# Layer 0's edge stage: running sums carried by a matmul with the identity, and copied out by ScalarE

## What is computed

```
e = einsum('ehd,ehd->eh', q[src], k[dst]) * scale
m = segment_max(e, dst);  ex = exp(e - m[dst]);  denom = segment_sum(ex, dst)
agg = segment_sum(ex / denom[dst] * v[src], dst)
```

## Time and profile before

| | |
|---|---|
| median of 3 runs | 6235.39 us (6235.18 to 6241.73) |
| the profiled execution | 6232.7 us |
| its span, first to last instruction | 6230.8 us |
| granted TensorE clock, mean of the span | 0.838 |
| the changed stage | about 727 to 2160 us, a quarter of the span |

### The profile page before, as it was taken

One profiled execution on the slowest core, in us unless ns is written; L12 is line 12 of the kernel. 1 busy time (PEld: TensorE's weight loads), 2 busy tenths in 40 slices (PEclk: granted clock), 3 DMA queues, 4 the chain that ended last, 5 costly groups with the idle time before them and its releaser, 6 DMA issues. The chain is left out here.

```text
span 6230.8 us, 86151 instructions
## 1 busy us (share of the span) xinstructions
PE 4655.4 (75%) x21453; PEld 3370.4 (54%) x21454; DVE 3982.9 (64%) x9527; ACT 2668.4 (43%) x5421; POOL 3080.8 (49%) x3260
## 2 busy tenths in 40 slices
PE   6977577777777697499999225566556659999999
PEld 4753255555555597366666215444444436666665
DVE  6864389999999777232222777777777764444443
ACT  1541055555555432154444212767776632222222
POOL 2767366666666487577777001777777720000000
PEclk7989899989899855599999557777777779999999
DMA  2014678888888686333232227555555530000000
GB/s 57 1 28 119 227 236 250 249 249 246 250 248 251 205 200 166 99 80 79 65 79 66 77 64 232 154 151 149 151 151 150 150 102 12 12 12 12 5 7 12
DMA packets 587385, 787.21 MB, mean 126 GB/s; under 512 B 207700, under 2 KB 427323, under 8 KB 586749
## 3 DMA queue, kind: packets, MB, share of 16 engines
q0 software_dynamic: 159136, 383.90, 23.0%
q1 hardware_dynamic: 290173, 351.82, 17.8%
q10 hardware_dynamic: 137972, 50.36, 3.3%
HBM read 634.22 MB, written 158.32 MB: 127 GB/s over the span
## 5 line engine op out<-in xcount | busy, mean ns | idle before, releaser
L1372 POOL DMA_INDIRECT b_got<-tmp_l_table,b_src x928 | 878.6, 947 | 505.8 <-issue 256.2
L2473 POOL DMA_INDIRECT w_got<-tmp_l_table,w_src x928 | 881.9, 950 | 284.4 <-issue 277.2
L3216 POOL DMA_INDIRECT t_got<-tmp_f_table,t_src x672 | 634.4, 944 | 220.4 <-issue 202.7
L1616 PE MATMUL b_pk<-b_keys,b_hot_t 128*128 x1856 | 532.9, 437 | 249.7 <-issue 157.2
L2736 PE MATMUL w_pa<-w_got,w_hot 128*128 128x264 f32 x1856 | 589.7, 471 | 98.8 <-DVE w_got L2643 96.5
L1616 PEld LDWEIGHTS b_pk<-b_keys,b_hot_t 128*128 128x128 f32 x1856 | 377.8, 214 | 335.2 <-issue 280.8
L3667 DVE SCALAR_TENSOR_TENSOR l_accs<-l_po,l_prob,l_accs 128x256 f32 (+1 forms) x392 | 173.5, 480 | 566.8 <-PE l_po L3776 566.8
L3719 ACT ACTIVATE l_h<-l_ph,l_bn 128x896 f32<-128x896 f32 x224 | 245.0, 1096 | 655.6 <-PE l_ph L3766 655.6
L2736 PEld LDWEIGHTS w_pa<-w_got,w_hot 128*128 128x128 f32 x1856 | 406.2, 231 | 205.2 <-issue 120.3
L1631 PE MATMUL b_pa<-b_got,b_hot 128*128 128x260 f32 x1856 | 487.7, 410 | 5.6 <-DVE b_acc L1543 4.8
L1631 PEld LDWEIGHTS b_pa<-b_got,b_hot 128*128 128x128 f32 x1856 | 387.0, 209 | 77.4 <-issue 7.0
(11 more groups left out here) (579 smaller groups left out, 9980.2 us busy)
## 6 DMA issues: line engine op xcount, KB each, us to landing
tmp_g_acc<-b_acc SPq DMA_DIRECT2D x232, 260.0 KB, 3.6
b_spread<-tmp_g_rel_rows SPq DMA_DIRECT2D x116, 256.0 KB, 5.3
w_spread<-tmp_g_rel_rows SPq DMA_DIRECT2D x116, 256.0 KB, 3.5
e_attr<-in_edge_attr ACTq DMA_DIRECT2D x103, 256.0 KB, 4.4
tmp_f_experts<-t_y SPq DMA_DIRECT2D x28, 896.0 KB, 4.5
t_spread<-tmp_f_rel_rows SPq DMA_DIRECT2D x174, 128.0 KB
yl_y<-tmp_f_experts SPq DMA_DIRECT2D x20, 896.0 KB, 11.2
b_got<-tmp_l_table,b_src POOLq DMA_INDIRECT x928, 4.5
```

The source lines that it names most:

```text
L1372: pool.indirect_dma_start(out=got[:, m % NB, u, :], out_offset=None, in_=T["l0_table"], in_offset=bass.IndirectOffsetOnAxis(ap=src[:, m * ...
L1616: mm = pe.matmul(pk[:, b % 2, u * D:(u + 1) * D], hot_t[:, (at * B4 + b) % HB, u * P:(u + 1) * P], keys[:, bass.ds(tile[u // 2], 1), :], s ...
L2473: pool.indirect_dma_start(out=got[:, p % 3, u, :], out_offset=None, in_=T["l1_table"], in_offset=bass.IndirectOffsetOnAxis(ap=src[:, p * R ...
L3216: pool.indirect_dma_start(out=got[:, g % RING, u, :], out_offset=None, in_=T["f_table"], in_offset=bass.IndirectOffsetOnAxis(ap=src[:, g * ...
```

## The change

The running sum is no longer made by VectorE. TensorE leaves a stop's bank open after the two sums (`sum_of_stop`) and adds a third matmul, `carry_of_stop`: the identity times one of six rows of `sums`, picked by a register: the four places of acc, faded_acc (4) or zeros (5). ScalarE copies the finished bank to acc (`collect`) and raises `added`. The row's number stands beside the numbers of tiles in a new table `orders`, 16 values a round, worked out once by VectorE from keep; TensorE loads all 16 at the head of a round. keep is loaded to one partition. TensorE's order interleaves carries and the next stop's sums; the last copy of a round (stop 7) opens ScalarE's next round; VectorE's `fade_last` moves behind score 0. The calls of the rounds get or lose the argument `two_behind`.

```diff
+    FADED, NONE = AS, AS + 1
...
-        keep = s.sb("keep", [P, L.stops])
+        keep = s.sb("keep", [1, L.stops])
+        orders = s.sb("orders", [1, ROUNDS + 1, 2 * RS], I32)
...
-        acc = s.sb("acc", [P, AS, WV])
-        faded_acc = s.sb("faded_acc", [P, WV])
+        sums = s.sb("sums", [P, AS + 2, WV])
+        acc, faded_acc = sums[:, 0:AS, :], sums[:, FADED, :]
...
-            sp.dma_start(keep[:, :], T[L.name + "_keep"].partition_broadcast(P)).then_inc(loaded, 16)
+            sp.dma_start(keep[:, :], T[L.name + "_keep"].rearrange("(a s) -> a s", a=1)).then_inc(loaded, 16)
+            sp.dma_start(orders[0:1, 0:ROUNDS - 2, 0:RS], T[L.name + "_i_row"][RS + 2:RS * (ROUNDS - 1) + 2]
+                         .rearrange("(a p s) -> a p s", a=1, s=RS)).then_inc(loaded, 16)
+            sp.dma_start(orders[0:1, ROUNDS - 2, 0:RS - 2], T[L.name + "_i_row"][RS * (ROUNDS - 1) + 2:L.stops]
+                         .rearrange("(a s) -> a s", a=1)).then_inc(loaded, 16)
...
+            def collect(p, n):
+                g = p * RS + n
+                if n % 2 == 0 and (not isinstance(p, int) or p or n >= AS):
+                    act.wait_ge(stored[n // 2 % 2], 16 * (RS // AS * p + n // AS))
+                act.wait_ge(summed, g + 1)
+                act.activation(acc[:, n % AS, :], pa[:, n % 2, 0:WV], ACT.Copy).then_inc(added, 1)
...
+                if two_behind:
+                    collect(p - 2, RS - 1)
...
+                collect_of(0)
                 if behind:
                     make_hot(p - 1, 2)
                     make_apart(p - 1, 3)
+                collect_of(1)
                 if two_ahead:
                     make_hot_t(p + 2, at + 2, 1)
+                collect_of(2)
...
+                collect_of(3)
+                collect_of(4)
+                if now_:
...
+                collect_of(5)
                 if two_ahead:
                     make_hot_t(p + 2, at + 2, 2)
+                collect_of(6)
...
+            dve.memset(sums[:, NONE, :], 0.0)
+            dve.wait_ge(loaded, 96)
+            for n in range(RS):
+                before = FADED if n == 0 else (n - 1) % AS
+                dve.tensor_scalar(orders[0:1, 1:ROUNDS + 1, RS + n], keep[0:1, :].rearrange("a (p s) -> a p s", s=RS)[:, :, n],
+                                  float(before - NONE), float(NONE), ALU.mult, ALU.add)
...
                 weigh_of(0)
-                if two_behind:
-                    add(p - 2, at - 2, RS - 2)
-                    add(p - 2, at - 2, RS - 1)
+                score_of(0)
                 if behind:
                     fade_last(p - 1)
-                score_of(0)
                 if now_:
                     spans(p)
...
+            def orders_of(p, a, b):
+                return values(orders[0:1, bass.ds(p, 1), a:b].rearrange("a p s -> a (p s)"))
...
+            def sum_of_stop(p, n, k):
+                g, b = p * RS + n, n // 2
+                pe.wait_ge(hot_ready, p * B4 + b + 1)
+                pe.wait_ge(rhs_ready, p * B4 + b + 1)
+                if not isinstance(g, int) or g >= 2:
+                    pe.wait_ge(added, g - 1)
+                for u in range(2):
+                    v = 2 * (n - 2 * b) + u
+                    pe.matmul(pa[:, n % 2, 0:WV], hot[:, b, v, :], got[:, k, v, D:ROW], start=(u == 0), stop=False)
+            def carry_of_stop(p, n, value):
+                before = nc.s_assert_within(value, 0, NONE, skip_runtime_bounds_check_because="it is worked out from a comparison's 0 or 1")
+                if n == 0:
+                    pe.wait_ge(faded, p + 1)
+                else:
+                    pe.wait_ge(added, p * RS + n)
+                pe.matmul(pa[:, n % 2, 0:WV], K["ident"][:, :], sums[:, bass.ds(before, 1), :], start=False, stop=True).then_inc(summed, 1)
...
-                    tile = tiles(p + 1, 2, 10 if two_ahead else 8)
+                first, last = 0 if ahead else RS, 2 * RS if behind else RS
+                if ahead and not two_ahead:
+                    tile, kept = orders_of(p, 0, RS - 2), orders_of(p, RS, 2 * RS)
+                else:
+                    found = orders_of(p, first, last)
+                    tile, kept = found[0:RS - first], found[RS - first:]
                 expand_of(1)
-                sums_of(0, 0, 1)
+                sum_of(0)
+                carry_of(0)
+                sum_of(1)
                 if now_:
                     chain_ends(p)
                 expand_of(2)
-                sums_of(1, 2, 3)
+                carry_of(1)
+                sum_of(2)
+                carry_of(2)
+                sum_of(3)
                 if now_:
                     spread_tops(p)
                 expand_of(3)
-                sums_of(2, 4, 5)
+                carry_of(3)
+                sum_of(4)
+                carry_of(4)
+                sum_of(5)
                 if now_:
                     turn_weights(p)
                 expand_of(4)
-                sums_of(3, 6, 7)
-
-            pe.wait_ge(loaded, 64)
+                carry_of(5)
+                sum_of(6)
+                carry_of(6)
+                sum_of(7)
+                carry_of(7)
+            pe.wait_ge(set_up, 2)
+            pe.wait_ge(loaded, 96)
             pe.wait_ge(keys_in[0], 16)
-            tile = tiles(0, 0, 10)
+            tile = values(i_row[0:1, 0:RS + 2])
```

More of the change, by code:

```diff
@@ L1400, in make_hot, with round_, collect_of @@
                 act.activation(hot[:, b, :, :], apart[:, b % 2, :, :], ACT.Relu, scale=-1.0, bias=K["ones"][:, 0:1]).then_inc(hot_ready, 1)
-            def round_(p, at, two_ahead, ahead, now_, behind):
+            def round_(p, at, two_ahead, ahead, now_, behind, two_behind):
+                def collect_of(n):
+                    if behind:
+                        collect(p - 1, n)
+                if two_behind:
+                    collect(p - 2, RS - 1)
                 if ahead:
@@ L1436, in _ @@
             act.wait_ge(set_up, 2)
-            round_(0, 0, True, True, True, False)
-            round_(1, 1, True, True, True, True)
+            round_(0, 0, True, True, True, False, False)
+            round_(1, 1, True, True, True, True, False)
             with act.Fori(0, TIMES) as i:
                 for c in range(LOOP):
[L1441 to L1444, removed]
+                    round_(LOOP * i + 2 + c, 2 + c, True, True, True, True, True)
+            round_(ROUNDS - 2, ROUNDS - 2, False, True, True, True, True)
+            round_(ROUNDS - 1, ROUNDS - 1, False, False, True, True, True)
+            round_(ROUNDS, ROUNDS, False, False, False, True, True)
+            round_(ROUNDS + 1, ROUNDS + 1, False, False, False, False, True)
         @block.vector
@@ L1530, in weigh, with round_ @@
                 dve.tensor_tensor(rows, rows, w.unsqueeze(3).broadcast_to((P, U, H, V)), ALU.mult).then_inc(rhs_ready, 1)
[L1532 to L1546, removed]
+            def round_(p, at, turn, ahead, now_, behind):
                 def weigh_of(b):
@@ L1554, in score_of @@
                         score(p + 1, at + 1, b, slot(at + 1, b), turn + (B4 * (at + 1) + b) // NB)
[L1556 to L1559, removed]
                 if behind:
@@ L1588, in _ @@
             done = link.here
-            round_(0, 0, 0, True, True, False, False)
+            round_(0, 0, 0, True, True, False)
             done = link.here - done
-            round_(1, 1, 0, True, True, True, False)
+            round_(1, 1, 0, True, True, True)
             with dve.Fori(0, TIMES) as i:
@@ L1594, in _, with values @@
                 for c in range(LOOP):
-                    round_(LOOP * i + 2 + c, 2 + c, i, True, True, True, True)
+                    round_(LOOP * i + 2 + c, 2 + c, i, True, True, True)
             link.leave(TIMES)
[L1597 to L1600, removed]
+            round_(ROUNDS - 2, ROUNDS - 2, 0, True, True, True)
+            round_(ROUNDS - 1, ROUNDS - 1, 0, False, True, True)
+            round_(ROUNDS, ROUNDS, 0, False, False, True)
         @block.tensor
         def _(pe):
-            def tiles(p, a, b):
-                return nc.values_load_multi_w_load_instructions(i_row[0:1, bass.ds(p * RS + a, b - a)], engines=[mybir.EngineType.PE],
+            def values(row):
+                return nc.values_load_multi_w_load_instructions(row, engines=[mybir.EngineType.PE],
                                                                 min_val=0, max_val=NT - 1, skip_runtime_bounds_check_because=WHY)[1]
+            def orders_of(p, a, b):
+                return values(orders[0:1, bass.ds(p, 1), a:b].rearrange("a p s -> a (p s)"))
             def expand(p, at, b, tile):
@@ L1618, in expand @@
                 mm.then_inc(expanded, 1)
[L1620 to L1629, removed]
-                        v = 2 * (n - 2 * b) + u
-                        mm = pe.matmul(pa[:, n % 2, 0:WV], hot[:, b, v, :], got[:, k, v, D:ROW], start=(u == 0), stop=(u == 1))
-                    mm.then_inc(summed, 1)
```

(9 more changed lines are left out.)

5 lines of the change are left out of this document (removed).

## The result

The changed kernel takes 6085.5 us (median of 4 runs, 6081.9 to 6090.6) beside 6235.3 us before (6229.1 to 6241.7): a ratio of 0.976, 95% interval 0.9743 to 0.9777. That is 150 us less, where 138 were forecast. The profiled execution's span is 6080.6 us, 150.2 less than in the earlier trace rows.

A forecast was written before the change was run, and what follows sets the result against it. VectorE was taken to bound the kernel at 23.68 us a round; TensorE's 14.4 + 3.5 + 1.4 + 1.6 + 0.4 us give 21.3. Over 57 rounds that saves 136 us, plus 3 at the start: 6097 us, range 6045 to 6225.

The forecast's parts named there:

- TensorE becomes the bound, VectorE gets slack: Stage's rounds: VectorE drops to 18.1 us of work, TensorE sets a round of 21.3 us, down from 23.68.
- The register load, 1.10 us: TensorE's load of 16 values at the round's head: 1.10 us if alignment sets the price, 3.87 at the other end.
- The head, 1.6 us: From the transpose's start to the first expansion on TensorE: shrinks from 2.43 to 1.6 us.
- Array work, 19.3 us: TensorE's round without waits: expansions and sums 14.4 us, carries 3.5, small matmuls 1.4.
- The carries' waits, 0.4 us: TensorE's carries waiting for ScalarE's copies: 0.4 us a round, bounds 0 and 8 x 0.5 us.
- Rival A: ScalarE's order and fuller queues eat half the gain, copies 0.3 us late: round 22.6 us, 6170 us; chance 0.18.
- Copy and ScalarE's load: ScalarE: 8 copies of 0.41 us a round, with other work and DMA issues 17.8 of 21.3 us.
- The clock: Lower granted clock after two of three round heads, costing up to 3.0 us on a full TensorE, expected to go.
- GpSimd's floor, 20.0 us: GpSimd's 16 gathers a round with their issue take 20.0 us, the next bound below 21.3.
- Start and end of the stage: Loads of keep's copies go, so the first round starts earlier: -3 us, between 0 and -6; the end was not priced.

The follow-up runs named there:

- e6: The changed kernel with eight useless 128 x 128 products, the last waited for, at the end of VectorE's round: 6101.4 us, ratio 0.9772.
- e4: The changed kernel with a second carry, the identity times the row of zeros, ahead of each real one: 6214.5 us, ratio 0.9958.
- e10: The changed kernel with half of round p + 3's spread rows issued in round p behind its first store, some 10 us earlier: 6059.5 us, ratio 0.9702.
- e1: The kernel before, TensorE's load of 8 values reading a copy shifted by two elements, so starting at multiples of 8: 6214.9 us, ratio 0.9956.
- e2: The changed kernel with its table of 16 values a round starting at element 2 of rows of 24: 6373.8 us, ratio 1.0212.
- e3: The changed kernel without the carries, so running sums are left out: 6020.2 us, ratio 0.9648.
- split load: The changed kernel loading 8 registers at the head, 8 behind the first expansion: 6089.8 us; with spread rows also issued earlier: 6033.5 us.
- e5: The changed kernel with VectorE instead of ScalarE copying the banks, at the old additions' places, and fade_last ahead of score 0: 6527.6 us, ratio 1.0461.

## Why the prediction was right, point by point

- **TensorE becomes the bound, VectorE gets slack**: right for VectorE (e6) and nearly so for TensorE (59.53 of 63.22 us; e4). TensorE's share was to be over 90% (94), VectorE's 85% (88). But TensorE's own path, its last carry's wait included, takes 20.42 us a round (e10); the last 0.63 of the 21.05 belong to the loop through the spread rows.
- **The register load, 1.10 us**: right, 1.107, and for the reason given (e1, e2). It was the largest risk of the forecast: the same change with the table two elements further on is 2.1% slower than before. The rule of the Trainium skill (Runtime: NRT & Kernel Launch, Instruction fetch mechanics) of about 200 ns a register would have given a round of 23.4 us. The Trainium skill's section speaks of register loads that the runtime puts in; those here are the kernel's own, from SBUF, and they lie below it at aligned addresses (74 and 69 ns a value in e1 and after, by 592/8 and 1107/16), and exceed it at others (242 and 284). The Trainium skill's floor of about 600 ns for a tensor load (DMA: Bandwidth & Descriptors, Latency and other measured facts) fits TensorE's 592 ns for 8 aligned values; ScalarE's 547 lie a little under it.
- **The head, 1.6 us**: 1.26. I let the load begin where it did before, 0.1 us after the transpose's start; on a full array it begins 0.24 us ahead of it on average, 0.41 in two rounds of three, and 0.71 in e4. Gain of 0.34 us unforeseen.
- **Array work, 19.3 us**: 19.0. Passes of 0.22 us were right; the small matmuls took 1.2, not 1.4, and sums and expansions together 14.3, not 14.4.
- **The carries' waits, 0.4 us**: half of what they were. 21.05 - 19.0 - 1.26 leaves 0.8 us. Of it 0.27 is the last carry of a round, in e10 as well: its only cover is one stop's sums, and copy 6 stands behind the pair of hot_t instructions, which the prediction named. The other 0.5 to 0.6 is the loop through the spread rows. The prediction saw its row ("no DMA wait on this path today but those for spread rows (3.0 us in three rounds)") and dismissed it: it asked only whether hot_t itself was wanted early ("each has most of a round of slack"), and not what stands behind hot_t on ScalarE. Now copies stand there. So the mechanism of Rival A was at work, at a third of its price. Two errors, 0.64 us too much in head and array and 0.4 too little in waits, left 0.25: that the round came out so close is in part luck.
- **Copy and ScalarE's load**: 0.368 us for 0.41; ScalarE busy 15.4 us a round and DMA issues beside it.
- **The clock**: right. 5 us at 1.2 GHz between the first and the last transpose, where the kernel before had 251. e2 shows the other direction: with heads of 4.7 us, 324 us of it.
- **GpSimd's floor, 20.0 us**: 19.86 (e3).
- **Start and end of the stage**: the start gave 1.0 us where 3 were credited; the end lost 3.5 us that were not priced. In the last round no expansions lie between the carries: from the carry at 1991.83 us to the one at 2004.56 a stop takes 1.59 us, 1.32 of it passes (four of sums and two of a carry) and the rest the bare chain from carry to copy to carry. The two errors are 5.5 us together. The rest of the program was 3.1 us shorter in the trace of the kernel after, which nothing here explains and which hides over half of them.

## What to carry to other kernels

When work moves to an engine that executes in order, ask not only whether each of its waits has slack for its own reader, but what now stands behind it. Where an edit that plainly shortens the full engine's path changes nothing, look for a longer loop through a transfer, break that first, and try the edit again: here the split load's 0.46 us a round came back only then. Lay tables from which registers are loaded so that each load starts at a multiple of 8 elements and takes whole eights.

## What the runs showed of the hardware

- A register load of 4-byte values into TensorE's sequencer takes 590 ns for 8 and 1107 for 16 from a start at a multiple of 8 elements, and 1937 for 8 and 4544 for 16 from a start 2 elements off. Only the offset of 2 was tried. Aligned loads of other counts cost more than full eights: 837 ns for 6 and 1278 for 10 (e1). SyncE's loads of 14 values were not varied and stay unexplained: in the trace of the kernel before, the one from element 0 took 1434 ns and the one from element 56 took 3142.
- TensorE's sequencer runs ahead of the array. The load begins 0.1 us behind the transpose's start (before), 0.24 ahead (after), 0.71 ahead (e4): in these three kernels, the more array work is queued without a wait, the more of the load is hidden. In e10 it is 0.41 us ahead in two rounds of three and 0.12 behind in the third, the first one in every pass of the loop over three rounds, with mean heads of 1.08 and 1.59 us. That this comes from the loop's branch was only argued.
- ScalarE took its instructions as written: in the timeline shown no copy passed the hot_t that waited 1.55 us. The Trainium skill says the same (PSUM — Partial Sum Buffer, Engine vs sequencer instructions: strictly first in, first out, on ScalarE, VectorE and GpSimd), and e5's VectorE agrees: the product stood behind a copy that waited 2.94 us.
- Idle time ahead of a weight load that the profile calls "issue" can be waiting for another engine: 74.2 us ahead of the carries fell to 26.3 when ScalarE was on time (after, e10).
